# A graph layer, linear attention and 64 experts on one core: the experts' list by one-hot products, router weights from two logits, more shared work beside the expert pairs, attention scores by pairs of pieces

## The reference

```python
xn = layernorm(x)
# graph attention, 8 heads of 32: exp(q.k/sqrt(32)) over the edges, sum per receiver, two dense layers
gnn = xn + relu(relu(relu(agg / denom) @ Wa + ba) @ Wf + bf)
# linear attention over all nodes, 8 heads of 64, elu + 1 as feature map
mix = (q @ (k.T v)) / (q @ sum(k)) @ Wo.T + bo
x = x + gnn + mix
z = layernorm(x); h = layernorm(z) * ln1_g + ln1_b
logits = h @ Wr @ codebook.T / 0.7                  # 64 experts
vals, idx = top_k(softmax(logits), 2)               # w = vals / sum(vals)
moe = sum over the two experts of w * (silu(h @ W1[e] + b1[e]) @ W2[e] + b2[e])      # W1 512x256
shared = 0.25 * (silu(h @ Ws1 + bs1) @ Ws2 + bs2)   # 1,024 hidden
hm = moe + shared
x = x + z + hm + (silu(layernorm(hm) @ Wf1 + bf1) @ Wf2 + bf2)
```

## Time and profile before

| | before |
| --- | --- |
| time, median of 3 runs | 962.72 us (960.28 to 964.75) |
| the profiled execution: its time, its span | 966.97 us, 965.2 us |
| busy: PE, DVE, ACT, POOL | 886.7 (92%), 526.9 (55%), 298.9 (31%), 165.8 us (17%) |
| granted clock of PE, mean | 0.975 of full speed |
| chain that ended last, by engine | PE 73%, DMA 9%, DVE 6%, issue 4%, ACT 4% |
| POOL's 20 scatters of the list | 23.7 us busy, 1.186 each |

### The profile page before, as it was taken

How to read it: one execution, slowest core, us unless ns; L and a number is a source line. 1 busy time by engine, 2 the same in 40 slices (tenths; PEclk the granted TensorE clock), 3 DMA queues, 4 the chain that set the end, 5 groups by cost and what they waited for, 6 DMA issues and landing times.

```text
span 965.2 us, 11954 instructions
## 1 busy us (share of the span) xinstructions
PE 886.7 (92%) x3946; PEld 488.1 (51%) x3946; DVE 526.9 (55%) x1371; ACT 298.9 (31%) x592; POOL 165.8 (17%) x199
## 2 busy tenths in 40 slices
PE   2899999799998999999999799999998999986898
PEld 1564454745586333333355486744654465443365
DVE  7785656755765899999955562032223222322382
ACT  2631101100104555555533441111221122111273
POOL 3000000500100000000000334622232223223240
PEclk9999999999998999999999799999999999997989
DMA  9201000000228240401001604259999899997522
GB/s 295 109 1 44 1 0 1 1 1 1 110 103 184 52 107 1 107 1 44 0 25 51 254 1 133 58 201 333 328 325 318 308 324 322 319 335 261 155 82 86
DMA packets 42043, 129.88 MB, mean 135 GB/s; under 512 B 9065, under 2 KB 9539, under 8 KB 41343
## 3 DMA queue, kind: packets, MB, share of 16 engines
q1 hardware_dynamic: 32955, 110.76, 35.6%
q0 software_dynamic: 8576, 18.03, 5.3%
q10 hardware_dynamic: 452, 0.34, 0.2%
HBM read 118.51 MB, written 19.71 MB: 143 GB/s over the span
## 4 chain that ended last, share of the span: by engine, by line
PE 73%; DMA 9%; DVE 6%; issue 4%; ACT 4%; POOL 2%; DVEq 1%; SPq 1%; ACTq 0%; POOLq 0%
PE ps L1475 10%; PE ps L1392 7%; PE ps L1464 7%; DMA Zg<-z_d,gat 7%; PE ps L1531 6%; PE ps L1543 5%; PE ps L1618 5%; PE ps L1636 4%; PE ps L1419 4%; PE ps L1428 4%; PE ps L1374 3%; PE ps L1360 3%; PE ps L1500 2%; PE ps L1686 2%; PE ps L1434 2%
## 5 line engine op out<-in xcount | busy, mean ns | idle before, releaser
L1037 DVE TENSOR_SCALAR hgT<-ps,cols 128x128 f32<-128x128 f32 x148 | 50.5, 403 | 147.7 <-PE ps L1608 147.6
L899 DVE TENSOR_TENSOR att<-ps,C 125x832 f32<-125x832 f32 (+1 forms) x120 | 121.8, 1017 | 13.5 <-ACT ps L1193 10.2
L1193 ACT ACTIVATE ps<-ps 125x832 f32<-125x832 f32 (+1 forms) x120 | 101.7, 849 | 71.3 <-PE ps L1464 71.3
L1475 PE MATMUL ps<-att,V 125*64 125x416 f32 (+1 forms) x480 | 111.2, 542 | 2.1 <-DVE att L899 1.6
L1269 ACT COPY eo<-ps 128x512 f32<-128x512 f32 x36 | 21.1, 586 | 199.5 <-PE ps L1636 199.5
L1464 PE MATMUL ps<-Qst,Kst 128*125 128x416 f32 (+1 forms) x240 | 77.2, 404 | 1.2 <-DVE C L856 0.7
L1464 PEld LDWEIGHTS ps<-Qst,Kst 128*125 128x125 f32 x240 | 35.6, 187 | 78.9 <-DVE att L899 71.4
L1618 PE MATMUL ps<-W,hgT 128*64 128x256 f32 x576 | 74.7, 404 | 0.7 <-DMA W<-in_W 0.6
L1531 PE MATMUL ps<-hT,Ws_s 128*128 128x250 f32 x320 | 72.4, 381 | 1.0 <-ACT combT L1252 1.0
L1543 PE MATMUL ps<-Ws_s,hsT 128*125 128x512 f32 x160 | 73.3, 598 | 0.0
L1392 PE MATMUL ps<-mW,xnT 128*125 128x512 f32 x160 | 72.2, 594 | 0.0
(11 more groups left out here) (241 smaller groups left out, 1241.9 us busy)
## 6 DMA issues: line engine op xcount, KB each, us to landing
W<-in_W SPq DMA_DIRECT2D x144, 512.0 KB, 6.3
Kst<-qk_d SPq DMA_DIRECT2D x32, 156.2 KB, 5.7
Qst<-qk_d SPq DMA_DIRECT2D x32, 156.2 KB, 5.9
Yt<-y_d SPq DMA_DIRECT2D x10, 448.0 KB
Ws_s<-in_Ws SPq DMA_DIRECT2D x2, 2048.0 KB, 14.2
qk_d<-qk_hi POOLq DMA_DIRECT2D x4, 625.0 KB, 3.6
qk_d<-qk_lo POOLq DMA_DIRECT2D x4, 625.0 KB, 4.7
z_d<-yz POOLq DMA_DIRECT2D x10, 250.0 KB, 2.7
```

The source lines that it names most:

```text
L899: V_.tensor_tensor(att[:, n % 3, :, 0:w], scores_of(n, w), C[:, s, o:o + w].unsqueeze(1).to_broadcast([P, 2, w]), ALU.mult).then_inc(att_m ...
L1037: i = V_.tensor_scalar(hgT[:, u, k, :], bank(u, 128, 128, k * 128), col("g1", k), col("b1ln", k), ALU.mult, ALU.add)
L1193: S_.activation(b, b, ACT.Exp, scale=float(DK) ** -0.5).then_inc(s_exp, 1)
L1475: k = MM(sums_of(i, 64 * j, 64, w), V[:, s, pair, j:j + 2, :], att[:, n % 3, j, 0:w], start=s == 0, stop=s == T - 1, skip_group_check=True)
```

## The change

Five edits in one step:

- **Attention by pairs of pieces.** PE issues scores(n + 2), scores(n + 3), sums(n), sums(n + 1).
- **Transposes and router.** Tiles 0 to 5 of yz are transposed between gnn_a and gnn_f of the last chunk; router chunk 0 stands before the transposes of tiles 6 to 9. hT is copied unscaled, one instruction per tile (ACT 8 tiles, DVE 2). g1 is multiplied into Wr instead, b1ln comes in through a vector rb (eight small matmuls and a copy in the linear attention's part); columns 0 to 499 of hT are scaled by ACT afterwards, the rest by POOL, for the shared network. Ws1 is fetched after attention instead of after the graph tiles.
- **Router weights from a gap.** The top two are taken from the logits; the weights are 1 / (1 + e) and e / (1 + e) with e = exp(second - first): one ACT instruction of 10 values instead of 10 of 64, and no division of the whole table.
- **The list by products.** DVE makes a one-hot of each position's row (rowhot, 20 x 128) and of its column (slots, 20 x 52), the latter once plain and twice times the upper and lower bits of the row's number; PE multiplies them in 20 matmuls of 156 columns, and DVE puts lst together from PSUM. list_d, its clearing, the 20 scatters and the read are gone.
- **More beside the pairs.** Hidden groups 0 to 5 stay ahead; 6 to 11 and shared tiles 0 and 1 join the parts given out over the 32 pairs. The ten additions of bf2 on POOL move from before the list into pairs 2 to 11, between scatter and next gather.

The core of the diff:

```diff
+    parts = []
+    for c, first in enumerate((8, 8, 12, 16)):
+        if c == 0:
+            parts += [("hidden", i, k) for i in (6, 7) for k in range(2)]
+        else:
+            parts += [("hidden", i, k) for i in range(first, first + 4) for k in range(2)]
+        parts += [("shared", t, k) for t in (2 * c, 2 * c + 1) for k in range(3)]
...
-            gp.dma_start(list_d.rearrange("(p n) o -> p (n o)", p=128), nobody[:, :]).then_inc(list_clear, 16)
-            gp.wait_ge(xy_kept, T)
-            for t in range(T):
-                nc.gpsimd.tensor_tensor(XR[:, t, :], XR[:, t, :], row("bf2"), ALU.add).then_inc(xy_kept, 1)
-            gp.wait_ge(list_clear, 16)
-
-            gp.wait_ge(pos_made, 1)
-            for k in range(TOPK):
-                for t in range(T):
-                    gp.indirect_dma_start(
-                        out=list_d, out_offset=bass.IndirectOffsetOnAxis(ap=posi[:, k, t:t + 1], axis=0),
-                        in_=toki[:, k, t:t + 1], in_offset=None).then_inc(list_made, 16)
-            gp.wait_ge(list_made, 16 * TOPK * T)
-
-            gp.dma_start(lst[:, 0:NP], list_d.rearrange("(p n) o -> p (n o)", n=NP)).then_inc(lst_in, 16)
-
+            gp.wait_ge(filled, TURNS.filled("rT", 2))
+            for k in range(KD):
+                nc.gpsimd.tensor_scalar(hT[:, k, 500:], hT[:, k, 500:], col("g1", k), col("b1ln", k), ALU.mult, ALU.add).then_inc(hT_scaled2, 1)
...
+                if 2 <= p < 2 + T:
+                    t = p - 2
+                    gp.wait_ge(xy_kept, T)
+                    nc.gpsimd.tensor_tensor(XR[:, t, :], XR[:, t, :], row("bf2"), ALU.add).then_inc(bf2_added, 1)
...
-            for t in range(1, T, 2):
...
+            for t in (8, 9):
...
+                V_.tensor_copy(hT[:, :, t * P:t * P + P], bank(TURNS.bank("hT", t), KD * P).rearrange("p (k n) -> p k n", k=KD)).then_inc(dve_read, 1)
...
-            V_.tensor_scalar(sm[:, 0, :], sm[:, 0, :], -1.0, None, ALU.mult)
-            v.drain().then_inc(lmax_made, 1)
-            v.wait_ge(prob_exp, T)
-            V_.reciprocal(sm[:, 1, :], sm[:, 1, :])
-            v.drain()
-            V_.tensor_tensor(prob[:, :, :], prob[:, :, :], sm[:, 1, :].unsqueeze(2).to_broadcast([P, T, E]), ALU.mult)
...
+                v.drain()
+                for t in range(5 * i, 5 * i + 5):
+                    V_.max(top8[:, t, :], prob[:, t, :])
...
+            V_.tensor_tensor(sm[:, 2, :].unsqueeze(2), top8[:, :, 1:2], top8[:, :, 0:1], ALU.subtract).then_inc(gap_made, 1)
...
+            V_.reciprocal(wtop[:, :, 0:1], sm[:, 2, :].unsqueeze(2))
...
+            V_.tensor_tensor(wtop[:, :, 1:2], wtop[:, :, 0:1], sm[:, 1, :].unsqueeze(2), ALU.mult)
...
+            V_.tensor_copy(posh[:, :, :], posw[:, 1:3, :])
+            v.drain()
+            V_.tensor_tensor(slots[:, :, 0, :], iotaQ[:, :].unsqueeze(1).to_broadcast([P, TOPK * T, NP]),
+                             posh[:, 1, :].unsqueeze(2).to_broadcast([P, TOPK * T, NP]), ALU.is_equal)
+            V_.tensor_tensor(rowhot[:, :, :], iotaR[:, :].unsqueeze(1).to_broadcast([P, TOPK * T, 128]),
+                             posh[:, 0, :].unsqueeze(2).to_broadcast([P, TOPK * T, 128]), ALU.is_equal)
+            v.drain()
+            for j in range(2):
+                V_.tensor_tensor(slots[:, :, 1 + j, :], slots[:, :, 0, :], idh[:, j, :].unsqueeze(2).to_broadcast([P, TOPK * T, NP]), ALU.mult)
+            v.drain().then_inc(slots_made, 1)
...
+            reads("list", 0)
+            b = TURNS.bank("list", 0)
+            V_.tensor_scalar(lf[:, :], bank(b, NP), -float(NOBODY), float(NOBODY), ALU.mult, ALU.add)
+            v.drain()
+            V_.tensor_tensor(lf[:, :], lf[:, :], bank(b, NP, 128, NP), ALU.add)
+            v.drain()
+            V_.tensor_tensor(lst[:, 0:NP], lf[:, :], bank(b, NP, 128, 2 * NP), ALU.add).then_inc(dve_read, 1)
...
+            a.wait_ge(gap_made, 1)
+            S_.activation(sm[:, 1, :], sm[:, 2, :], ACT.Exp).then_inc(gap_exp, 1)
...
-            for n in range(SETS * T):
-                if n + 2 < SETS * T:
-                    scores(n + 2)
+            for n in range(0, SETS * T, 2):
+                for k in (n + 2, n + 3):
+                    if k < SETS * T:
+                        scores(k)
                 sums(n)
+                sums(n + 1)
...
+            def z_transposed(tiles):
+                for t in tiles:
+                    pe.wait_ge(z_made, t + 1)
+                    b = turn("hT", t)
+                    for k in range(KD):
+                        i = nc.tensor.transpose(bank(b, P, 128, k * P), yz[:, t, k:D:KD], ident[0:P, 0:P])
+                    i.then_inc(filled, 1)
...
+                if c == 2:
+                    z_transposed(range(6))
...
+            router(0, 3)
+            z_transposed(range(6, T))
+            router(1, 7)
+            router(2, 9)
...
-            whole_hidden(5)
-            pe.wait_ge(comb_made, 1)
-            for c, (t0, n) in enumerate(((0, 4), (4, 4), (8, 2))):
-                b = turn("combT", c)
-                for t in range(n):
-                    i = nc.tensor.transpose(bank(b, P, E, t * P), prob[:, t0 + t, :], ident[0:P, 0:P])
-                i.then_inc(filled, 1)
-            read_by_now("combT", 2)
-            whole_hidden(6)
...
+            whole_hidden(3)
+            pe.wait_ge(comb_made, 1)
+            for c, (t0, n) in enumerate(((0, 4), (4, 4), (8, 2))):
+                b = turn("combT", c)
+                for t in range(n):
+                    i = nc.tensor.transpose(bank(b, P, E, t * P), prob[:, t0 + t, :], ident[0:P, 0:P])
+                i.then_inc(filled, 1)
+            whole_hidden(4)
+            pe.wait_ge(slots_made, 1)
+            b = turn("list", 0)
+            for n in range(TOPK * T):
+                i = MM(bank(b, 3 * NP), rowhot[:, n, :], slots[:, n, :, :].rearrange("p s q -> p (s q)"), start=n == 0, stop=n == TOPK * T - 1)
+            i.then_inc(filled, 1)
+            whole_hidden(5)
```

More of the change, by code:

```diff
@@ L105 @@
     ("hidden", ["act"]),
+    ("owner", ["dve"]),
+    ("hidden", ["act"]),
     ("combT", ["act"] * 3),
     ("hidden", ["act"]),
-    ("owner", ["dve"]),
-    ("hidden", ["act"]), ("shared", ["dve"] * 2), ("hidden", ["act"] * 4), ("fb", ["dve"]),
+    ("list", ["dve"]),
+    ("hidden", ["act"]), ("fb", ["dve"]),
 ]), (2, 6, [
-    ("shared", ["dve"] * 2),
+    ("hidden", ["act"] * 2), ("shared", ["dve"] * 2),
+    ("hidden", ["act"] * 4), ("shared", ["dve"] * 2),
     ("hidden", ["act"] * 4), ("shared", ["dve"] * 2),
@@ L142, in parts_beside @@
 def parts_beside():
-    parts = ([("shared", t, k) for t in (2, 3) for k in range(3)]
-             + [("hidden", i, k) for i in range(12, 16) for k in range(2)] + [("shared", t, k) for t in (4, 5) for k in range(3)]
-             + [("hidden", i, k) for i in range(16, 20) for k in range(2)] + [("shared", t, k) for t in (6, 7) for k in range(3)])
+    parts = []
[5 more added lines that the diff above has]
+        parts += [("shared", t, k) for t in (2 * c, 2 * c + 1) for k in range(3)]
     cost = {"hidden": 4 * 250, "shared": 3 * 512}
@@ L1247, in _ @@
             a.wait_ge(z_out, 16 * T)
-            for i in range(6):
+            for i in range(4):
                 shared_hidden(i)
+                if i:
+                    keep_sum(6 + i)
             for c, tiles in enumerate(((0, 4), (4, 4), (8, 2))):
@@ L1252, in _ @@
                 S_.copy(combT[:, tiles[0] * P:(tiles[0] + tiles[1]) * P], bank(TURNS.bank("combT", c), tiles[1] * P, E)).then_inc(act_read, 1)
-            for i in range(6, 12):
+            for i in range(4, 6):
                 shared_hidden(i)
@@ L1549, in whole_hidden @@
                     shared_hidden(i, half)
-            for i in range(5):
+            for i in range(2):
                 whole_hidden(i)
@@ L1597, in _ @@
             i.then_inc(filled, 1)
+            read_by_now("combT", 2)
+            read_by_now("hidden", 5)
+            read_by_now("list", 0)
             read_by_now("fb", 0)
-            read_by_now("owner", 0)
-            read_by_now("hidden", 11)
-            read_by_now("shared", 1)
             def transposes(p, g, u):
```

157 lines of the change are left out of this document (84 added, 73 removed).

## The result

| | before | after |
|---|---|---|
| median of 4 runs each, us | 961.62 (960.28 to 964.75) | 934.92 (933.49 to 935.96) |
| ratio of the times | | 0.9702, 95% interval 0.9664 to 0.9741 |
| profiled execution, us | 966.97 | 934.68 |
| busy share of PE | 92% | 93% |

The change makes the kernel 3.0% faster. The forecast was 946 with a range from 935 to 955. The sign was right; the medians lie 26.7 us apart where 16.7 were summed, and the time lies 0.1 us under the range. A later set of 6 runs of the changed kernel gave 0.9681 (0.9644 to 0.9719).

A forecast was written before the change was run, and what follows sets the result against it. TensorE, busy 92% of the span, was taken as the bound. The terms -5.5 - 8.6 + 3.7 - 6.6 + 0.3 = -16.7 us against the profiled 966.97 gave 950.3, scaled to the median 946; range 935 to 955.

The forecast's parts named there:

- Attention, -5.5: Attention stage: ordering scores and sums by pairs of pieces saves 5.5 us, bounds 0 and -8.
- The pairs, -6.6: The 32 pairs: more parts beside them cut TensorE's waits for gathers, saving 6.6 us, bounds 0 and -10.
- Transposes and router, -8.6: Last graph tiles to logits: earlier transposes and router chunk 0 at full clock save 8.6 us, from -5 to -9.
- The list, +3.7: Front, logits to first pair: list by one-hots and matmuls, less the work moved beside the pairs, costs 3.7 us.
- the 29 that the forecast had named as a sign of failure: Front: the forecast is wrong if slots_made comes over 29 us after the logits.
- Small things, +0.3: rb's matmuls and copy, Wr's scaling and the earlier Ws1 load, in earlier stages, together cost 0.3 us.
- all behind the pairs, 0: End of the kernel: the last four pairs and all behind them stay as they are.
- Rival 4: More than the sum: 3.4 us more in the pairs, 4 to 5 elsewhere as half-clock stretches go; 938 us, chance 0.08.
- Rival 2: The pairs gain nothing, since the bf2 sums delay ten gathers: 952.5 us, chance 0.14.
- Rival 3: Attention gains nothing: a change of kinds costs the same, or the new order takes it back; 951.5 us, chance 0.11.
- Rival 5: Slower: attention's blocks run in series and DVE waits in each of 60; 976 us at 0.5 more each, chance 0.03.
- Rival 6: No change, 958 to 964 us: Rival 2 and Rival 3 together, and slots_made later than bounded; chance 0.04.

The follow-up runs named there:

- b_again: The kernel before, unchanged, profiled a second time: 962.72 us.
- the two swaps: Only TensorE's order in attention swapped: old order in the kernel after, 946.70 us; order by pairs of pieces in the kernel before, 952.58 us.
- a_beside_less: Kernel after with hidden parts 6 to 11 and shared tiles 0 and 1 back in front of the pairs: 951.73 us, ratio to before 0.9871.
- a_bf2_out: Kernel after with POOL's ten bf2 additions in front of the pairs instead of among them: 944.92 us, ratio to before 0.9793.
- a_router_old: Kernel after with the old order of transposes and router, folded scale and bias and the reads kept: 932.53 us, ratio to before 0.9650.
- a_hT_scaled: Kernel after with its new order, but transposed tiles read by four scaling operations each and router weights unscaled: 933.63 us, ratio to before 0.9698.
- a_pool_late: Kernel after with POOL's scaling of hT behind its first two gathers instead of in front of the list: 933.64 us, ratio to before 0.9668.
- a_front: Kernel after with POOL's scaling of hT behind the first gathers and two moves in DVE's order (combine products, owner's reads): 934.93 us, ratio to before 0.9697.
- a_again: The kernel after, unchanged, measured and profiled again: 933.01 us, ratio to before 0.9681.
- a_tail_more: Kernel after with POOL's scaling of hT behind the first gathers and two thirds each beside pairs 30 and 31: 927.62 us, ratio to before 0.9625.

## Where the forecast failed, and where it held

The direction was right; two terms of the sum came out at twice their size. Each alone would have left the time inside the range. Together they are 5.5 and 5.9 us too small, and 946 less 11.4 is 934.6, just under the range's low end of 935. The other misses, counted against b_again, whose 962.72 us is the median that the forecast was scaled to, are -1.9 (router), +2.2 (list), -1.3 (last four pairs) and +0.6 (behind them). That they nearly cancel is luck.

**Attention, -5.5: the step that failed.** The sum on PE was right to the hundredth (2.50 a block, 2.51 measured), and the mechanism is shown by four runs. What failed is "from 320 to 476 us it waited for ScalarE's (ACT's) exponentials 4.2 us in all. That is what it can give back there". The term came out at 11.0 us (8.6 to 12.1 in the two swaps), outside its bounds of 0 and -8. Two things were missed. First, the list of waits leaves out short ones: in the same 156 us DVE was busy 143.4 (the profile of before), so it was idle 12.6 and not 4.2. Second, DVE's busy time was taken as fixed. Between b_again and after the stage lost 11.3 us: 6.3 of them idle time of DVE (172.84 - 155.50 against 161.56 - 150.50) and 5.0 busy time, with the same 230 instructions. Most of the 5.0 is overlap: the time in which two of its instructions run at once grew from 4.7 to 8.3 us. The other way round, not all idle time could be had: of the 19.3 us in the earlier trace rows, 11.1 are left after.

**The pairs, -6.6: the other term mis-sized.** It measured -12.5, outside its bounds of 0 and -10. The mechanism (parts cover the round from result to gathered rows) held, and a_beside_less shows it. Two steps were too careful. The sums on POOL were said to ask for more cover in pairs 2 to 11; a_bf2_out shows they cost nothing there. And of the 11.1 us of listed waits 4.5 were said to remain, where 1.2 did; PE's whole idle time, 13.5 us in b_again, is what fell, to 1.7.

**Transposes and router, -8.6: right in size, wrong in cause.** The stage gained 9.2 us against the first profile of before and 10.5 against the second. But the term was put down to the new order, with the copies as a detail of it. a_router_old and a_hT_scaled show that the order and the copies each suffice for nearly all of it. The rest of the step stands: the half clock went with the wait in front of it.

**The list, +3.7.** It measured +4.5 and +5.9 against the two profiles of before. This is the balance of the stage: no run puts the scatters or the softmax back alone, so what each of these two edits costs or gives is not shown. The one-hots took 1.24 + 2.82 + 2.40 = 6.5 us (6 taken), the 20 list matmuls 1.54 (2.0 taken), PE's waits 4.7. The list's one-hots were ready at +31.0 us, past the 29 that the forecast had named as a sign of failure, and the first pair came at +38.2 instead of +34 to +36. The half clock on hidden group 2 is most of the first and about half of the second: in a_router_old, whose code is that of after from the logits on and whose group 2 took 3.64 us, they came at +27.8 and +36.6; with POOL's scaling moved as well (a_pool_late, a_front) at +27 and at +34.6 and +35.2. Contention of DVE with POOL, 1.2 us here, was not counted either.

**Small things, +0.3, and all behind the pairs, 0.** Neither can be told from the spread: what is ahead of attention took 303.6 to 307.7 us in the profiles of both kernels. The last four pairs stayed; the 4 us that the first two profiles show there are no more than the spread between executions, which was tested and not assumed.

**Rivals.** Rival 4, more than the sum (938, chance 0.08), is the nearest in number. It had 3.4 us more in the pairs, where 5.9 came, but the rest from half-clock stretches that go in the front and the pairs, and the front still had one, on hidden group 2; attention's 5.5 it did not have. Rivals 2, 3, 5 and 6 are excluded by the runs, and with 3 the rule of the Trainium skill (TensorE: Matmul & The Clock Gate, Step-by-step: what each phase is for) by which a change of kind would cost nothing here: 1.41 us a piece stayed with DVE relieved, and only the order made it 1.25.

## What to carry to other kernels

A list of waits is no measure of an engine's idle time: it showed 4.2 us where 12.6 were idle. Take the idle time (length less busy time) as the upper bound of what that engine can give back, expect less, and check whether the new order also changes its busy time. When a change cures a wait by two means, undo each alone before naming a cause; here either would have done. Before a few microseconds in a short stretch are explained, profile the old kernel a second time.

## What the runs showed of the hardware

Some DVE operations on operands in SBUF stretch while POOL reads and writes SBUF: a scaling from 0.17 to 1.03 us, products from 0.83 to 1.36 and 1.80 us. Others do not: the searches for the experts' places (FIND_INDEX8) took 0.22 us each beside POOL's scaling in after and 0.22 in b_again. The Trainium skill (SBUF — State Buffer, Who interferes with whom) says that a DVE instruction with two inputs in SBUF contends with a POOL instruction that reads SBUF, that a scaling can contend too, and that the shared pair of ports is an exclusive lock; for a lock on the whole instruction the rows speak too, since short operations of DVE ended together with POOL's sums (546.44 and 546.40 us), and POOL's own sums took up to 1.84 us instead of 1.26 beside DVE's long products. Ten sums of POOL cost 9 to 10 us beside DVE's chain, and nothing in the pairs.

The half clock does not fall on the same place in each execution. Windows of a_again and then of a_tail_more, up to attention and attention itself; both kernels have the same instructions up to there:

```profile
0.00:307.72 307.72, 270.08 (x1181) 167.95 (x1181) 203.75 (x703) 62.71 (x109) 25.37 (x31) 0.98 0.20 62
307.72:469.20 161.48, 158.52 (x721) 64.33 (x721) 150.47 (x230) 96.41 (x120) 0.00 (x0) 1.00 0.25 56
```

```profile
0.00:303.62 303.62, 264.71 (x1181) 162.60 (x1181) 203.46 (x703) 62.71 (x109) 25.37 (x31) 1.00 0.19 61
303.62:469.38 165.76, 161.14 (x720) 65.27 (x720) 150.56 (x230) 96.42 (x120) 0.00 (x0) 0.98 0.25 57
```

The granted clock of 0.98 stands ahead of attention in the one and in it in the other; 4 us change their stage and in these two the sum stays. The hidden group behind base took 6.64 us in after and 3.64 in a_pool_late. The length of one of these stages from one profile is known to no better than that.
